# A recurrent layer ahead of a mixture of experts: first groups routed one by one, unit 0's rows turned before the last h

## The reference, cut to what matters

```python
# x: (8, 512, 128): 8 steps of the recurrence, 512 rows each
xp = x @ w + bias
for s in range(8):                                   # LSTM, H = 128
    g = xp[s] + h @ u
    i, f, o = sigmoid(g[:, :384]) in thirds; cand = tanh(g[:, 384:])
    c = f * c + i * cand
    h = o * tanh(c); hs[s] = h
x = layernorm(x + hs)                                # 8 groups of 512 tokens
logits = x @ router_w                                # 8 experts
top-2 gates of softmax(logits); each token's place in its expert's
list of C = 128 slots comes from a running count inside its group
expert_inputs = dispatch(x)                          # per expert and group 128 rows
hidden = gelu(expert_inputs @ w0[e]) * (expert_inputs @ w1[e])   # H = 688
out = combine(hidden @ wo[e], gates)
x = layernorm(x + out)
```

## Time and profile before

| | |
|---|---|
| time, 3 runs | 306.52 us (306.25 to 306.61) |
| span of the profiled execution | 342.1 us |
| PE busy | 293.1 us (86%) |
| DVE busy | 251.6 us (74%) |
| ACT busy | 217.3 us (64%) |
| POOL busy | 186.6 us (55%) |
| moved by DMA | 37.20 MB, mean 109 GB/s |

### The profile page before, as it was taken

The page is one execution under the profiler, slowest core; times in us unless marked ns, Lnnn a source line. Parts: engine busy times, 40 slices in busy tenths (PEclk is TensorE's granted clock), DMA queues, the critical chain, the costliest instruction groups (busy, mean ns, idle before and its releaser), DMA issues.

```text
span 342.1 us, 5646 instructions
## 1 busy us (share of the span) xinstructions
PE 293.1 (86%) x1692; PEld 244.8 (72%) x1692; DVE 251.6 (74%) x794; ACT 217.3 (64%) x495; POOL 186.6 (55%) x153
## 2 busy tenths in 40 slices
PE   8999999697754695529999999999999999998880
PEld 6666665496744695419999987877888888888770
DVE  2789989599621585026888889889877776996985
ACT  4689887665720473026777876877765566566884
POOL 5012788887777027787773433437436536559500
PEclk9999999999885598557999999999999999999996
DMA  6996582486521015324443326344214227325265
GB/s 218 363 407 167 127 251 74 99 229 191 166 89 57 22 28 151 97 35 47 49 62 57 52 46 175 76 113 64 47 16 63 33 19 134 65 36 86 24 163 153
DMA packets 46685, 37.20 MB, mean 109 GB/s; under 512 B 7057, under 2 KB 40784, under 8 KB 46656
## 3 DMA queue, kind: packets, MB, share of 16 engines
q1 hardware_dynamic: 35392, 26.56, 26.1%
q0 software_dynamic: 11264, 10.29, 19.6%
HBM read 17.86 MB, written 17.10 MB: 102 GB/s over the span
## 4 chain that ended last, share of the span: by engine, by line
PE 67%; DVE 10%; issue 7%; ACT 6%; another core or an unknown queue 5%; POOL 3%; DMA 1%; SPq 0%; ACTq 0%; DVEq 0%
PE big L647 11%; PE big L645 11%; PE big L646 10%; PE big L552 6%; PE b_ht L664 3%; PE b_xnt L661 2%; PE b_xnt L664 2%; PE b_xnt L662 2%; PE b_ht L661 2%; PE b_ht L662 2%; PE big L538 2%; POOL tokens L494 2%; PE b_rt L681 2%; PE big L539 2%
## 5 line engine op out<-in xcount | busy, mean ns | idle before, releaser
L834 ACT ACTIVATE act_g<-big 128x256 f32<-128x256 f32 (+1 forms) x144 | 65.0, 452 | 90.8 <-PE big L647 59.6
L645 PE MATMUL big<-x_hi,e_hi 128*128 128x256 f32 (+1 forms) x264 | 89.5, 339 | 0.3 <-issue 0.3
L647 PE MATMUL big<-x_lo,e_hi 128*128 128x256 f32 (+1 forms) x264 | 86.9, 329 | 1.3 <-issue 1.3
L646 PE MATMUL big<-x_hi,e_lo 128*128 128x256 f32 (+1 forms) x264 | 86.9, 329 | 1.0 <-issue 1.0
L479 POOL DMA_INDIRECT slots<-rows,slot_ix x64 | 68.5, 1071 | 33.6 <-issue 18.5
L494 POOL DMA_INDIRECT tokens<-contrib,token_ix x32 | 51.4, 1607 | 42.2 <-DVE token_ix L1108 34.4
L494 POOL DMA_INDIRECT tokens<-zero_rows,token_ix x28 | 45.2, 1614 | 35.5 <-DVE token_ix L1108 27.5
L646 PEld LDWEIGHTS big<-x_hi,e_lo 128*128 128x128 f32 x264 | 52.9, 200 | 4.5 <-issue 1.1
L647 PEld LDWEIGHTS big<-x_lo,e_hi 128*128 128x128 f32 x264 | 52.7, 199 | 4.4 <-issue 0.4
L645 PEld LDWEIGHTS big<-x_hi,e_hi 128*128 128x128 f32 x264 | 53.0, 201 | 3.7 <-issue 0.2
L1116 DVE TENSOR_TENSOR term_i<-act_g,big 128x256 f32<-128x256 f32 (+3 forms) x36 | 18.3, 508 | 17.4 <-ACT act_g L834 12.0
(11 more groups left out here) (204 smaller groups left out, 672.9 us busy)
## 6 DMA issues: line engine op xcount, KB each, us to landing
e_raw<-in_L_ffn_w_kernel_dram SPq DMA_DIRECT2D x16, 320.0 KB
slots<-zero_rows SPq DMA_DIRECT2D x8, 548.0 KB, 7.6
e_raw<-in_L_ffn_wo_kernel_dram SPq DMA_DIRECT2D x8, 320.0 KB
xd<-slots SPq DMA_DIRECT2D x16, 137.0 KB
xd<-slots SPq DMA_DIRECT2D x8, 274.0 KB
e_lo<-e_raw POOLq DMA_DIRECT2D x4, 544.0 KB
x<-in_L_attn_input_seq_dram SPq DMA_DIRECT2D x8, 256.0 KB, 4.5
tokens<-rows SPq DMA_DIRECT2D x8, 256.0 KB
```

Of the source, the lines that this page charges most:

```text
L645: pe.matmul(dst, e_hi[q][:, c0:c0 + m], xdt_hi[u % 2][:, 0:w], start=True, stop=False)
L646: pe.matmul(dst, e_lo[q][:, c0:c0 + m], xdt_hi[u % 2][:, 0:w], start=False, stop=False)
L647: mm = pe.matmul(dst, e_hi[q][:, c0:c0 + m], xdt_lo[u % 2][:, 0:w], start=False, stop=True)
L834: nc.scalar.activation(act0[n % RH][0:m, 0:w], pre(n, P)[0], ACT.Gelu_apprx_tanh).then_inc(gelu_ready, 1)
```

## The change

**Routing parts.** The batches 0 to 3 become the parts r = 0 to 4: group 0, group 1, and then three batches of two groups. `ROUTED_IN` has part 0 in step 2, part 1 in step 3, part 2 (groups 2 and 3) in step 5 as before. The ops of parts 0 and 1 have half the width.

**POOL.** The scatters of group 0 start after step 2. `power(2)` and the second `low_half` of expert 0 move in among the scatters, and all later `power`s to other tiles.

**The turn.** PE turns unit 0's rows right behind the last `h_part` (in the bank `b_xt`, where it was `big[3]`), the two `keep_warm(8)` go, and `turn_sum(7)`, `places` of the third batch and `logits(7)` move among unit 0's chunks. ACT splits these rows ahead of the last `tanh_c`. DVE does `shift(5)`, `scale_less`, `low_xd(0)` and group 6's `stat`, `moment` and `variance` ahead of the last h, and the rest of the third batch's routing later among the chunks than before.

```diff
-    LOWS_AMONG = {(1, 0): (1, 0), (1, 1): (1, 1)}
-    ROOTS_AMONG = {(0, 2): 3, (0, 5): 4, (1, 0): 5, (1, 2): 6, (1, 3): 7}
+    LOWS_AMONG = {(0, 6): (0, 1), (1, 0): (1, 0), (1, 1): (1, 1)}
+    ROOTS_AMONG = {(0, 3): 2, (0, 5): 3, (0, 7): 4, (1, 2): 5, (1, 4): 6, (1, 5): 7}
+    ROUTED_IN = {2: 0, 3: 1, 5: 2}
...
+        def batch_of(r):
+            return max(r - 1, 0)
+        def groups_of(r):
+            return range(r, r + 1) if r < GB else range(GB * (r - 1), GB * r)
...
-            for s in range(3):
-                if s == 2:
-                    low_half(0, 0)
+            for s in range(2):
                 power(s)
-            low_half(0, 1)
-            for b in range(NB):
-                scatter(b, range(BT))
+            low_half(0, 0)
+            for r in range(NR):
+                scatter(r)
...
             for s in range(1, S):
                 h_part(s)
+                if s == S - 1:
+                    turn_xd(0)
                 turn_sum(s - 1)
...
-                if s >= 3 and s % 2 == 1 and s < S - 1:
-                    places(s // 2 - 1)
-            pe.wait_ge(gate_read, gate_no(S - 1, 2))
-            keep_warm(8, big[2])
-            turn_xd(0)
-            turn_sum(S - 1)
-            keep_warm(8, big[2])
+                if s in ROUTED_IN:
+                    places(ROUTED_IN[s])
...
-                    if (u, k) == (0, 1):
-                        places(NB - 2)
-                    elif (u, k) == (0, 2):
+                    if (u, k) == (0, 3):
+                        turn_sum(S - 1)
+                    elif (u, k) == (0, 4):
+                        places(NR - 2)
+                    elif (u, k) == (0, 5):
                         logits(S - 1)
...
-                if s >= 3 and s % 2 == 1 and s < S - 1:
-                    exp(s // 2 - 1)
+                if s in ROUTED_IN:
+                    exp(ROUTED_IN[s])
+                if s == S - 1:
+                    high_xd(0)
...
+                if s == S - 1:
+                    shift(S - 3)
+                    scale_less(NR - 2)
+                    low_xd(0)
+                    stat(S - 2, range(T))
+                    moment(S - 2)
+                    variance(S - 2)
                 dve.wait_ge(tanh_ready, s + 1)
...
             sum_y(S - 1)
-            stat(S - 2, range(T))
-            moment(S - 2)
-            variance(S - 2)
-            shift(S - 3)
-            scale_less(NB - 2)
-            low_xd(0)
             for n in range(5):
-                gate_step(NB - 2, n)
-            slot_base(NB - 2)
-            void_base(NB - 2)
+                gate_step(NR - 2, n)
+            chunk(0, 0)
+            slot_base(NR - 2)
+            void_base(NR - 2)
+            chunk(0, 1)
+            shift(S - 2)
+            low_weights(2, 0)
+            chunk(0, 2)
             stat(S - 1, range(T))
             moment(S - 1)
             variance(S - 1)
+            chunk(0, 3)
+            assign(NR - 2, 0)
+            assign(NR - 2, 1)
             best(S - 2)
```

More of the change, by code:

```diff
@@ L341, in b_xd @@
         def b_xd(u):
-            return b_xt if u else big[3]
+            return b_xt
         def piece(n):
@@ L466, in low_half, with scatter @@
                 pool.dma_start(e_lo[e][:, cols], e_raw[e % 2][:, cols], accum_op=ALU.add).then_inc(elo_in[e], 16)
-            def scatter(b, tiles):
+            def scatter(r):
+                b = batch_of(r)
                 pool.wait_ge(zeros_out[b], 16 * GB)
-                pool.wait_ge(slot_step, AS * (b + 1))
-                pool.wait_ge(gate_rows_in, b + 1)
-                for t in tiles:
+                pool.wait_ge(slot_step, AS * (r + 1))
+                pool.wait_ge(gate_rows_in, r + 1)
+                for t in range(tiles_of(r).start, tiles_of(r).stop):
                     if (b, t) in ROOTS_AMONG:
@@ L569, in logits, with places @@
                 mm.then_inc(logits_ready, 1)
-            def places(b):
-                pe.wait_ge(chosen_ready, b + 1)
-                for g in range(GB):
-                    lo, pl = g * T, place_ps(b)[:, g]
+            def places(r):
+                pe.wait_ge(chosen_ready, r + 1)
+                for g in groups_of(r):
+                    lo, pl = g % GB * T, place_ps(batch_of(r))[:, g % GB]
                     pe.matmul(pl[:, 0:T, :, :], before[:, :], chosen[:, lo:lo + T, :, :], start=True, stop=True)
@@ L755, in norm_rows, with high_xd @@
                                          bias=root_b[:, q, t:t + 1], scale=root_y[:, q, t:t + 1]).then_inc(xn_ready, 1)
+            def high_xd(u):
+                act.wait_ge(xdt_ready, u + 1)
+                if u >= 2:
+                    act.wait_ge(pre_ready, (2 * FULL + 1) * (u - 1))
+                nc.scalar.activation(xdt_hi[u % 2][:, 0:width(u)], b_xd(u)[:, 0:width(u)], ACT.Copy).then_inc(xdhi_ready, 1)
             for s in range(S):
@@ L1001, in assign_batch @@
                 else:
-                    dve.wait_ge(slot_step, AS * b + n)
+                    dve.wait_ge(slot_step, AS * r + n)
                 if n == 1:
-                    for g in range(GB):
+                    for g in range(gs.start, gs.stop):
                         ins = dve.tensor_tensor(place[:, g * T:(g + 1) * T, :, :], place_ps(b)[:, g, 0:T, :, :],
@@ L1028, in low_weights, with low_xd @@
                                   ALU.subtract).then_inc(elo_ready, 1)
+            def low_xd(u):
+                dve.wait_ge(xdhi_ready, u + 1)
+                w = width(u)
+                dve.tensor_tensor(xdt_lo[u % 2][:, 0:w], b_xd(u)[:, 0:w], xdt_hi[u % 2][:, 0:w], ALU.subtract).then_inc(xdlo_ready, 1)
             for s in range(S):
-                b = s // 2 - 1
-                routes = s >= 3 and s % 2 == 1 and s < S - 1
+                routes, r = s in ROUTED_IN, ROUTED_IN.get(s)
                 if s >= 1:
@@ L1043, in _ @@
                 if routes:
-                    scale_less(b)
+                    scale_less(r)
                 dve.wait_ge(gate_read, gate_no(s, 2))
@@ L1186, in _ @@
             variance(S - 1)
+            chunk(0, 3)
+            assign(NR - 2, 0)
+            assign(NR - 2, 1)
             best(S - 2)
-            shift(S - 2)
-            low_weights(2, 0)
-            chunk(0, 0)
-            assign_batch(NB - 2, 0)
-            assign_batch(NB - 2, 1)
-            chunk(0, 1)
-            assign_batch(NB - 2, 2)
-            assign_batch(NB - 2, 3)
-            chunk(0, 2)
-            shift(S - 1)
-            assign_batch(NB - 2, 4)
-            assign_batch(NB - 2, 5)
-            chunk(0, 3)
-            low_weights(2, 1)
-            gate_values(NB - 2)
-            gate_row(NB - 2)
-            chunk(0, 4)
-            best(S - 1)
+            low_weights(2, 1)
+            chunk(0, 4)
+            shift(S - 1)
+            assign(NR - 2, 2)
+            assign(NR - 2, 3)
             chunk(0, 5)
             low_weights(2, 2)
-            for k in range(3):
-                chunk(1, k)
-            scale_less(NB - 1)
+            assign(NR - 2, 4)
+            assign(NR - 2, 5)
+            chunk(1, 0)
+            gate_values(NR - 2)
+            gate_row(NR - 2)
+            chunk(1, 1)
+            best(S - 1)
+            chunk(1, 2)
+            scale_less(NR - 1)
             low_weights(2, 3)
```

152 lines of the change are left out of this document (78 added, 74 removed).

## The result

The changed kernel takes 312.25 us (311.05 to 312.92, 4 runs) against 306.38 us for the kernel before (306.18 to 306.61, 4 runs): ratio 1.0194, 95% interval 1.0161 to 1.0226, 5.9 us slower. The direction was right; the forecast, 308.4, was 3.9 us too low, and the time lies outside the range, 304.8 to 311.0.

What follows compares the result with a forecast made beforehand. PE, full from 160 to 290 us, bounds the kernel, so its arrival in unit 2 counts; DVE is close in the recurrence and binds at the turn. 1.4 + 3.4 + 1.1 - 3.6 - 0.4 = +1.9, so 308.4 us, range 304.8 to 311.0.

Steps and rivals of the forecast that it cites:

- Part 1: Group-by-group routing: more DVE work between h of step 2 and h of step 3 makes PE wait, +1.4 us.
- Part 2: Second low_half of expert 0 issued later, so expert 2's weights land late and hold h of step 6, +3.4 us.
- That wait stays just hidden: Unit 0's rows, loaded about 63 and needed at 66, would not make the kernel wait.
- Part 3: PE's lower clock: 0.8 us on the last h products after the wait for h, 0.3 in unit 0; +1.1 us.
- the clock in full: Rival: all last h products at 1.2 GHz, 3.4 us not 0.8; unit 0 1.0 not 0.3; 311.7 us, chance 0.17.
- The 0.3 for unit 0: Lower clock from PE's gaps in unit 0 without keep_warm, mostly hidden behind DVE: 0.3 us.
- Part 4: The turn, last cell to low_xd(2): reordered DVE work fills waits, -4.0, with one new gelu wait, +0.4; -3.6 us.
- Part 5: Batch 0's last scatter and batch 1's come earlier, so PE no longer waits for unit 3's rows, -0.4 us.
- Part 2's upper bound: Expert 2's weights landing at 62 us, making the late load cost 5.9 us.
- POOL's powers are late instead: Rival: late weights hidden, DVE waits for power(5), 1.0 us, and power(6), 1.2 us; 306.8 us, chance 0.13.
- Faster: Rival: POOL at 1.28 us a scatter, expert 2's weights there at 56.2, powers not late; 304.3 us, chance 0.20.

Runs made afterwards that it cites:

- the kernel with the early low half: Changed kernel with the second low_half of expert 0 ahead of tile 3 of group 0 instead of tile 6 of batch 0: 306.56 us, ratio 0.9985.
- the second trace of before: The kernel before, run and profiled once more with no edit: 306.76 us, span 304.6.

## Why the prediction was right in its direction and wrong in its size

**Part 1, +1.4: right.** h of step 3 starts at 34.86, 1.5 us later, with PE waiting 0.6; the 1.5 stays through step 5.

**Part 2, +3.4: the mechanism was right, the term mis-sized; it measured 6.2.** POOL's and SP's starts were met within 0.3 us. Two numbers failed. The load was priced at 5.7 us from a load in the experts' stage; here it takes 7.7, as the two low halves of expert 1 run beside it. I had moved the second `low_half` of expert 0 and not asked what the now late load would meet. That is 2.0 us. And h of step 6 stood 0.87 us late in the execution that I read, behind waits of 0.17 and 0.52 us that the other trace doesn't have; I subtracted this late h, so the wait in the sum came out that much too short. "That wait stays just hidden" failed by 0.64 us: the load of unit 0's rows came at 66.37 and not about 63.

**Part 3, +1.1: mis-sized.** The h products cost 2.5 us more, not 0.8. The price was a quarter of the full 3.4; nothing in the rows asked for a quarter, and the rival "the clock in full" named this term. The rule of the Trainium skill ("TensorE: Matmul & The Clock Gate", section on HAM oscillation), that products behind an idle stretch run throttled, makes it the 3.4 that the prediction worked out; the trace lies between, nearer to the rule. The 0.3 for unit 0 did not come in this execution, where the clock is at 1.00 from 72 us on; the kernel with the early low half has a fall there, 0.50 from 80 to 82 us, and so has the kernel before at the turn.

**Part 4, -3.6: right within its bounds or a little better.** From the last `cell` to `x_lo` of unit 2 it is -4.2 us against the second trace of before; against the one in the prediction's rows (86.51 - 62.19 = 24.32, now 21.36) -3.0. The bounds were -4.0 to -2.5. The two traces of before agree from the last `cell` to the start of `low_xd(0)` (6.27 and 6.28 us) and part behind it, where the clock is low in one of them, so the difference is most likely the clock. In the kernel with the early low half the same stretch gained 2.7 us, with two waits for powers in it or ahead of it.

**Part 5, -0.4: the mechanism was right, the term mis-sized; it measured -2.0.** Behind `x_lo` of unit 2 PE's wait for unit 3's rows, 1.44 us in the second trace of before, is gone, and one wait ahead of it is 0.54 shorter (1.15 against 1.69).

The sum as measured is 1.5 + 6.2 + 2.5 - 4.2 - 2.0 = 4.0 in the two traces, and 1.6 us more by the medians, which no part accounts for. The range failed for a reason of its own: it moved one term at a time. Part 2's upper bound alone, 5.9, gives 310.9, the clock's rival alone 311.7, and both went up together, as the second follows from the first. The rivals: "POOL's powers are late instead" gave 306.8 for a kernel whose weights are in time, and the early low half measures 306.56. The time agrees partly by luck: the rival wanted 1.0 us for `power(5)` and 1.2 for `power(6)`, and the trace has 0.21 and 0.94, with 0.94 for `power(3)` that nobody had priced. The clock's rival came nearest to the time, 311.7, but for a part of the reason: it had the h products at 3.4 instead of 2.5 and left part 2 at 3.4 instead of 6.2. "Faster" needed the weights before 58.3; they landed at 61.8.

## What to carry to other kernels

When a transfer is moved, price what it runs beside in its new place: here the delayed load met two adding transfers, and its duration went from 6.2 to as much as 11.3 us with its lead on them. A wait behind which dense products follow has a second price, the clock: here 2.5 of the 3.4 us that the lower clock could cost, behind a wait of 6.1. When one term causes another, move both together for the range. And compare traces with the times of their own executions, not with medians. Moving one entry of a queue's list by three tiles was worth all of the loss, and another entry by one tile the only gain: after a reordering look at each in-order queue for the one entry that is now late.
